# A four-layer gated cross-attention kernel: the first feed-forward layer keeps the inner values of three pairs of tiles instead of two

## The chip, the cores and the metric

The kernel runs on one core of a Trainium2 chip. The metric is the device time of one execution, in microseconds (us). The engines of the core work side by side, each through its own list of instructions in order, and meet only at semaphores: TensorE (PE in the rows; PEld is its weight load), VectorE (DVE), ScalarE (ACT), GpSimd (POOL), and the queue of SyncE that issues transfers (SPq).

## What is computed

The input x is 4 batches of 512 tokens of width 128. Four layers follow one another, and each adds a gated cross-attention over 77 context tokens and then a gated feed-forward part. The change touches the feed-forward part of the first layer alone, whose linear maps quantise both operands to a 4-bit grid in blocks of 16:

```python
def fp4_quant_dequant(x):                      # per block of 16 along the last dim
    scale = max(max|xb| / 6, 1e-12)
    q = GRID[searchsorted(MID, |xb / scale|)] * sign(xb) * scale
def L0_ffn(x, w_gate, w_up, w_down):           # 128 -> 352 -> 128
    gate = fp4_linear(x, w_gate)
    y    = fp4_linear(x, w_up)
    h    = silu(gate) * y
    return fp4_linear(h, w_down)               # h is quantised here
x = x + tanh(g_ffn[0]) * L0_ffn(layernorm(x), ...)
```

## The kernel before, in words

The 2048 tokens are 16 tiles of 128 tokens. The first feed-forward layer (`ffn0`, one function of that name for each of TensorE, ScalarE and VectorE) works on 8 pairs of tiles, j = 0 to 7; i is a tile, i = 2j or 2j + 1. For each pair these steps follow one another:

1. TensorE, `up(i)` (L1747, L1748): the gate values of a tile into bank i % 2 of PSUM, the up values into bank 2 + i % 2. It first waits until the product of the pair before has read the banks (`h_done`).
2. ScalarE, `silu(i)` (L850): the silu of the gate values into `fsg`, one buffer for each tile of a pair.
3. VectorE, `product(j)` (L1326): `h` = up values times silu, for both tiles at once (128 x 704), into `fh[:, j % 2]`; then the maximum of each block of 16 (L1330).
4. VectorE, `rounded(j)`: three small operations for the scales (L981 to L983), and five of 128 x 704 that round to the grid (L973 to L977), from `fh[:, j % 2]` into the work buffer `qh[:, j % 2]`.
5. GpSimd (L677): `qh` times the scale, written back into `fh[:, j % 2]`; it signals `hq_done`.
6. TensorE, `turn(i)` (L1755): three transposes of the tile's part of `fh` into bank 4; it signals `hqT_ps`.
7. ScalarE, `hT_out(i)` (L854, L855): bank 4 into `hqT[:, i % 2]`.
8. TensorE, `down(i)` (L1764): six matmuls that accumulate the output of the tile.

So `fh` has two uses for each pair: VectorE writes the raw values and reads them for the rounding, and then GpSimd puts the quantised values in the same place, from where TensorE transposes them. With two buffers, the product of pair j has to wait until the two tiles of pair j - 2 have been transposed:

```python
dve.wait_ge(silu_done, 2 * j + 2)
if j >= 2:
    dve.wait_ge(hqT_ps, 2 * j - 2)
dve.tensor_tensor(h, ps[:, 2:4, 0:FI], fsg[:, :, :], ALU.mult).then_inc(h_done, 1)
```

The order of work is written out by hand on each engine, by rounds. In round j TensorE issues `up(2j)`, `up(2j+1)`, then `turn(2j-4)`, `down(2j-5)`, `turn(2j-3)`, `down(2j-4)`, so pair j - 2 is transposed behind the up projections of pair j; each `turn` after the first waits until ScalarE has copied the one before out of bank 4. In rounds 5 and 7 the first two batches of the next layer's attention are put in between (a transpose of the input, L1579, and the query projection, L1584). ScalarE issues the two silus of pair j, then the copies of pair j - 2. VectorE issues `product(j)` and `rounded(j)`, and in between: behind the product of pair 1 the quantisation of the last batch's input; behind `rounded(3)` and `rounded(5)` the residual of batch 0 and 1 (L1344, statistics, and a refinement of 1/sqrt); ahead of that of batch 1, and behind the last pair, the low part of the queries (L1207).

Behind the last pair VectorE takes the row maxima of the next layer's attention scores (L1217), 8 units of scores, then the residual of batch 2, 8 more units, and the residual of batch 3. TensorE writes a unit of scores (L1605, L1608, L1609) into bank 0 or 1 in turn, so it is at most two units ahead of the maxima. It issues the first 8 units in round 9, ahead of the last two `turn`s, and the other 8 behind the last `down`.

The buffers live in a region of SBUF that later stages use again. `fh` is followed there by `fsg`, `hqT`, `w1s`, `w2s`, and then by `qh`, whose space is afterwards that of the mask parts `m1hB`, `m1lB` and of `gap2`, a filler that nothing reads. When all of them are given up (`early.close()`), `cT`, `rk1`, `rk2` and the expert weights of the last layer are laid over the same region from its start.

Of the kernel before, what the change touches and what calls it, by code (L numbers as in the profile page):

```python
# [19 lines left out]
P = 128  # L20
# [7 lines left out]
FI = 352  # L28
# [66 lines left out]
def program(nc, a, out):  # L95
    with ExitStack() as ctx:
        def sb(name, shape, dt=F32):
            return ctx.enter_context(nc.sbuf_tensor(name, shape, dt))
# [4 lines left out]
        ps = ctx.enter_context(nc.psum_tensor("ps", [P, 8, 512], F32))  # L103
# [5 lines left out]
        ident = sb("ident", [P, P])  # L109
# [92 lines left out]
        def early_sb(name, shape, dt=F32):  # L202
            return early.enter_context(nc.sbuf_tensor(name, shape, dt))
# [5 lines left out]
        wst = early_sb("wst", [P, 3, 3, P])  # L209
        wqt = early_sb("wqt", [P, 2, FI])  # L210
        wdT = early_sb("wdT", [P, 3, P])
        fh = early_sb("fh", [P, 2, 2, FI])
        fsg = early_sb("fsg", [P, 2, FI])
        hqT = early_sb("hqT", [P, 2, 3, P])
        w1s = early_sb("w1s", [P, F1])
# [2 lines left out]
            qh = lent.enter_context(nc.sbuf_tensor("qh", [P, 2, 2, 2 * FI], F32))  # L218
        m1hB = early_sb("m1hB", [P, 2, S], F32R)
        m1lB = early_sb("m1lB", [P, 2, S], F32R)  # L220
        early_sb("gap2", [P, 768])
        early.close()
        cT = sb("cT", [TPB * NE, 2, P])
        rk1 = sb("rk1", [P, TPB * NE * NE], BF16)
# [274 lines left out]
        def _(pool):  # L499
# [131 lines left out]
            for l in range(L):  # L631
                for k in range(-2, B + 1):
                    n = l * B + k
                    if l == 0 and k == 1:
                        quantise_begun(2)
                        quantise_ended(2)
                    if 0 <= k < B and n + 2 < N and n + 2 >= 3 * B:
                        mask_rows(n + 2)
                    if 0 <= k < B and n + 3 < N:
                        key_rows(n + 3)  # L640
                    if 0 <= k + 1 < B:
                        split_maxima(n + 1)
                    if l == 0 and k == 0:
                        for j in range(2):
                            quantise_begun(j)
                            quantise_ended(j)
                    if l == 0 and k >= 2:
                        quantise_begun(k + 1)
                        quantise_ended(k + 1)
                    if l == 2 and k == -1:  # L650
                        refine((5, B - 1))
                        shift((5, B - 1))
                    if l == 2 and k == -1:
                        pool.wait_ge(am_w_part, 1)
                        pool.partition_all_reduce(am[:, 3:4], am[:, 1:2], P, RMAX).then_inc(am_w_all, 1)
                    if l == 0 and k in (-1, 1, 3):
                        mask_parts((k + 1) // 2)
                    if l == 1 and k in (-1, 0, 2):
                        mask_parts((3, 4, 0, 5)[k + 1])
                    if l == 1 and k == 1:  # L660
                        last_masks()
                    if l == 2 and k == 0:
                        split_experts(gH, gL, 0)
                    if l == 2 and k == 1:
                        split_experts(uH, uL, 1)
                    if k >= 1:
                        refine((2 * l + (l > 1) + 1, k - 1))
                        if l == 0:
                            shift((1, k - 1))
                    if l == 3 and 1 <= k <= 3:  # L670
                        split_down(k - 1)
                if l == 0:
                    for j in range(T // 2):
                        h = fh[:, j % 2, :, :].rearrange("p t (n e) -> p (t n) e", e=16)
                        v = qh[:, j % 2, 0, :].rearrange("p (n e) -> p n e", e=16)
                        pool.wait_ge(hq_scaled, j + 1)
                        pool.tensor_tensor(h, v, hscale[:, j % 2, :].unsqueeze(2).to_broadcast([P, 44, 16]),  # L677
                                           ALU.mult).then_inc(hq_done, 1)
                if l == 1:
                    for m in LN_ORDER[4 * B:6 * B]:  # L680
                        if m not in OWN and m != (5, B - 1):
                            refine(m)
                            shift(m)
                if l == 2:
                    pool.wait_ge(am_part, 1)
                    pool.partition_all_reduce(am[:, 2:3], am[:, 0:1], P, RMAX).then_inc(am_all, 1)
                if l == 3:
                    for n, (b, e) in enumerate(STEPS):
                        if e < NE:
                            k = b * NE + e  # L690
                            pool.wait_ge(s3_done, n + 1)
                            pool.wait_ge(cb_in[k % CRING], 16 * (k // CRING + 1))
                            pool.tensor_tensor(sg[:, n % 3, :], sg[:, n % 3, :], cb[:, k % CRING, :], ALU.mult).then_inc(sc_done, 1)  # L693
# [274 lines left out]
        def _(dve):  # L968
# [10 lines left out]
            def quant_scales(s, inv):  # L979

                link(dve.tensor_scalar(s, s, 1.0 / 6.0, 1e-12, ALU.mult, ALU.max))  # L981
                link(dve.reciprocal(inv, s))
                return dve.tensor_scalar(inv, inv, 1.0 - 2.0 ** -22, None, ALU.mult)  # L983
# [335 lines left out]
            def ffn0(q_rest, maximum):  # L1319
                def product(j):  # L1320

                    h = fh[:, j % 2, :, :]
                    dve.wait_ge(silu_done, 2 * j + 2)
                    if j >= 2:
                        dve.wait_ge(hqT_ps, 2 * j - 2)
                    dve.tensor_tensor(h, ps[:, 2:4, 0:FI], fsg[:, :, :], ALU.mult).then_inc(h_done, 1)  # L1326
                    dve.wait_ge(h_done, j + 1)
                    if j >= 2:
                        dve.wait_ge(hq_done, j - 1)
                    link(dve.tensor_reduce(hscale[:, j % 2, :], h.rearrange("p t (n e) -> p (t n) e", e=16), AX_X, ALU.max,  # L1330
                                           apply_absolute_value=True))

                def rounded(j):

                    v = fh[:, j % 2, :, :].rearrange("p t (n e) -> p (t n) e", e=16)
                    w = [qh[:, j % 2, i, :].rearrange("p (b e) -> p b e", e=16) for i in range(2)]
                    link(quant_scales(hscale[:, j % 2, :], qs[:, 1, :]))
                    quant_steps(w, v, qs[:, 1, :].unsqueeze(2).to_broadcast([P, 44, 16])).then_inc(hq_scaled, 1)
                    dve.wait_ge(hq_scaled, j + 1)
# [161 lines left out]
        def _(pe):  # L1501
# [227 lines left out]
            def ffn0(turn_input, queries, scores):  # L1729
# [20 lines left out]
                def turn(i):  # L1750
                    pe.wait_ge(hq_done, i // 2 + 1)
                    if i >= 1:
                        pe.wait_ge(hqT_ready, i)
                    for c, (f0, fw) in enumerate(FQ):
                        ins = pe.transpose(ps[0:fw, 4, c * P:(c + 1) * P], fh[:, i // 2 % 2, i % 2, f0:f0 + fw], ident[:, :])  # L1755
                    ins.then_inc(hqT_ps, 1)

                def down(i):
# [250 lines left out]
```

## Time and profile before

| What | us |
|---|---|
| Median of 3 runs | 832.74 (832.41 to 835.34) |
| The profiled execution, its own time | 834.32 |
| Its span, from the first to the last instruction | 832.5 |
| VectorE busy | 543.0 (65% of the span) |
| TensorE matmul busy | 638.8 (77%) |
| ScalarE busy | 326.1 (39%) |
| GpSimd busy | 261.4 (31%) |
| The first feed-forward layer: the product of pair 0 starts | 137.93 |
| The last of its products starts | 208.40 |

The mean clock that TensorE was granted is 0.844 of full speed (2.4 GHz); it has two levels, 1.0 and 0.5 (1.2 GHz), and a slice between them holds some of each. In a row of a timeline, the bracket at the end says how long the engine was idle before the instruction and what ended that; "x3" behind a row is that many instructions in one row, with the time of all of them together. Ends of matmuls are modelled. A row of the waits says who waited for whom, how long in total, how many times, and how long at most.

### The profile page before, as it was taken

What the parts mean: (1) busy time and instruction counts of PE and PEld (TensorE: products, weight loads), DVE (VectorE), ACT (ScalarE), POOL (GpSimd) and SP (SyncE); (2) the same over time, 40 slices, a digit from 0 to 9 for tenths busy, and PEclk for the clock granted to TensorE, in tenths of its full rate; (3) what the DMA queues carried; (4) which work ended last, traced back from release to release, by engine and by line L of the source; (5) the groups of instructions that cost most, each with busy time, mean ns of one, the idle gap of its engine ahead of it and who ended that gap; (6) DMA issues with size and microseconds to landing.
All of it is one profiled execution on the core that took longest, in us unless ns stands there. A gap on an engine that the chain in (4) does not pass through costs nothing. (4 is left out here: it accounts for less than half of the span.)

```text
span 832.5 us, 9949 instructions
## 1 busy us (share of the span) xinstructions
PE 638.8 (77%) x2926; PEld 397.5 (48%) x2926; DVE 543.0 (65%) x1451; ACT 326.1 (39%) x627; POOL 261.4 (31%) x470
## 2 busy tenths in 40 slices
PE   5788775566779998884888870348887898989997
PEld 3433333354665564552534330124343576767875
DVE  8775635888772553485736655863558798878655
ACT  3044552233224344353143440214544455545554
POOL 4343365111011312113250721001122445445463
PEclk9577987688869999896599985555998899999999
DMA  8864311002204323006044320222500232333341
GB/s 253 187 177 132 73 37 46 2 0 64 63 12 140 90 41 91 1 1 182 9 123 156 57 76 0 62 64 67 169 6 2 63 103 93 103 113 106 112 121 57
DMA packets 67989, 67.71 MB, mean 81 GB/s; under 512 B 25119, under 2 KB 48223, under 8 KB 67552
## 3 DMA queue, kind: packets, MB, share of 16 engines
q1 hardware_dynamic: 61326, 64.61, 28.4%
q10 hardware_dynamic: 6610, 2.47, 1.2%
q8 instruction: 24, 0.39, 0.2%
q14 instruction: 29, 0.24, 0.1%
HBM read 50.29 MB, written 17.60 MB: 82 GB/s over the span
## 5 line engine op out<-in xcount | busy, mean ns | idle before, releaser
L783 ACT ACTIVATE PT<-ps 110x512 f32<-110x512 f32 x192 | 110.5, 595 | 137.3 <-PE ps L1645 63.4
L1217 DVE TENSOR_REDUCE mraw<-ps 128x4 f32<-128x308 f32 x256 | 116.0, 476 | 73.6 <-PE ps L1605 23.7
L1605 PE MATMUL ps<-KG,QG 98*128 98x308 f32 x256 | 113.0, 477 | 49.4 <-DVE mraw L1217 34.1
L693 POOL TENSOR_TENSOR sg<-sg,cb 128x512 f32<-128x512 f32 x64 | 83.8, 1312 | 78.3 <-ACT sg L945 74.9
L1605 PEld LDWEIGHTS ps<-KG,QG 98*128 98x128 f32 x256 | 59.2, 237 | 94.4 <-DVE mraw L1217 70.4
L1645 PE MATMUL ps<-QG,KG 128*110 128x512 f32 x192 | 93.1, 506 | 9.1 <-ACT PT L783 6.7
L1461 DVE TENSOR_TENSOR ps<-ps,sg 128x512 f32<-128x512 f32 x72 | 50.3, 698 | 39.3 <-POOL sg L693 36.3
L1665 PE MATMUL ps<-PT,VN 128*18 128x512 f32 x512 | 73.0, 644 | 0.0
L525 POOL CAST mhl<-mraw 128x64 fp32r<-128x64 f32 x16 | 5.0, 310 | 192.7 <-DVE mraw L1217 180.0
L945 ACT ACTIVATE sg<-ps 128x512 f32<-128x512 f32 x72 | 43.0, 597 | 46.4 <-PE ps L1864 45.7
L1645 PEld LDWEIGHTS ps<-QG,KG 128*110 128x110 f32 x192 | 35.0, 187 | 54.4 <-ACT PT L783 38.8
L932 ACT ACTIVATE hH<-ps 128x512 fp32r<-128x512 f32 x72 | 43.0, 597 | 37.7 <-DVE ps L1461 36.2
L582 POOL TENSOR_TENSOR nt<-nhv,rs 128x4 f32<-128x4 f32 (+1 forms) x63 | 14.8, 236 | 129.9 <-DVE rs L1057 126.6
L1107 DVE RECIPROCAL rden<-ps 128x32 f32<-128x32 f32 x32 | 11.3, 354 | 64.3 <-PE ps L1555 64.2
L1453 DVE TENSOR_TENSOR hL<-ps,hH 128x512 fp32r<-128x512 f32 x72 | 49.0, 681 | 0.7 <-ACT hH L932 0.6
L724 ACT ACTIVATE xn<-x,nsh,rs 128x128 f32<-128x128 f32 x64 | 26.3, 482 | 44.2 <-DVE nsh L1072 22.4
L1747 PE MATMUL ps<-wqt,xnT 128*128 128x352 f32 x32 | 19.0, 690 | 28.8 <-DVE fh L1326 28.1
L1882 PE MATMUL ps<-hH,dwH 128*128 128x512 f32 x72 | 29.7, 413 | 1.2 <-ACT hH L932 1.2
L677 POOL TENSOR_TENSOR fh<-qh,hscale 128x704 f32<-128x704 f32 x8 | 11.1, 1385 | 59.6 <-DVE qh L977 59.6
L1884 PE MATMUL ps<-hL,dwH 128*128 128x512 f32 x72 | 29.3, 406 | 0.0
L1883 PE MATMUL ps<-hH,dwL 128*128 128x512 f32 x72 | 29.2, 405 | 0.0
L1079 DVE TENSOR_SCALAR xn<-x,mv,rs 128x128 f32<-128x128 f32 x64 | 22.3, 412 | 9.5 <-POOL rs L585 9.4
(284 smaller groups left out, 1414.9 us busy)
## 6 DMA issues: line engine op xcount, KB each, us to landing
cb<-c_parts SPq DMA_DIRECT2D x64, 256.0 KB, 3.3
QG<-q_parts SPq DMA_DIRECT2D x48, 256.0 KB, 3.9
KG<-k_parts SPq DMA_DIRECT2D x48, 154.0 KB, 3.0
q_parts<-hiT SPq DMA_DIRECT2D x14, 256.0 KB, 2.0
q_parts<-loT SPq DMA_DIRECT2D x14, 256.0 KB, 2.3
k_parts<-kmH SPq DMA_DIRECT2D x16, 154.0 KB, 2.4
k_parts<-kmL SPq DMA_DIRECT2D x16, 154.0 KB, 2.6
VN<-v_parts SPq DMA_DIRECT2D x16, 144.0 KB, 2.9
```

Source lines behind the costliest of these rows:

```text
L693: pool.tensor_tensor(sg[:, n % 3, :], sg[:, n % 3, :], cb[:, k % CRING, :], ALU.mult).then_inc(sc_done, 1)
L783: act.activation(PT[0:w, q % PTR, :], ps[0:w, 4 + q % 2, :], ACT.Exp, scale=SCALE[l]).then_inc(exp_done, 1)
L932: act.activation(hH[:, n % 3, :], ps[:, up_bank(n), :], ACT.Copy).then_inc(h_hi, 1)
L945: act.activation(sg[:, n % 3, :], ps[:, n % 2, :], ACT.Silu).then_inc(s3_done, 1)
L1217: dve.tensor_reduce(mraw[:, n % 2, i, g * HG:(g + 1) * HG], ps[:, u % 2, 0:GK].rearrange("p (h k) -> p h k", k=K), AX_X, ALU.max).then_inc ...
L1453: dve.tensor_tensor(hL[:, n % 3, :], ps[:, up_bank(n), :], hH[:, n % 3, :].bitcast(F32), ALU.subtract).then_inc(h_lo, 1)
L1461: dve.tensor_tensor(ps[:, up_bank(n), :], ps[:, up_bank(n), :], sg[:, n % 3, :], ALU.mult).then_inc(a1_done, 1)
L1605: ins = pe.matmul(o, QG[0:KS, n % 3, g, q], KG[0:KS, n % 3, g, :], start=True, stop=l not in (1, 2))
L1645: ins = pe.matmul(o, KG[:, n % 3, g, r], QG[:, n % 3, g, :], start=True, stop=l not in (1, 2))
L1665: pe.matmul(ps[p0:p0 + VC, 6 + f, :], VN[:, n % 3, g * 4 + PAIRS.index((t, j)), :], PT[:, q % PTR, :], start=s == 0, stop=s == 1, skip_gro ...
L1882: pe.matmul(o, dwH[:, e, :], hH[:, r, :], start=e == NE, stop=False)
L1884: pe.matmul(o, dwH[:, e, :], hL[:, r, :], start=False, stop=e == NE - 1).then_inc(f3_step, 1)
```

## The change

`fh` gets a third buffer. The product, the rounding, GpSimd's scaling and the transposes all index it with j % 3 in place of j % 2, and the product of pair j now waits for the transposes of pair j - 3. The work buffer `qh` and the scales stay at two. The filler `gap2` shrinks by the 704 values that `fh` grows by, and all buffers between the two move up by 2816 bytes in each partition.

```diff
-        fh = early_sb("fh", [P, 2, 2, FI])
+        fh = early_sb("fh", [P, 3, 2, FI])
...
-        early_sb("gap2", [P, 768])
+        early_sb("gap2", [P, 64])
...
-                        h = fh[:, j % 2, :, :].rearrange("p t (n e) -> p (t n) e", e=16)
+                        h = fh[:, j % 3, :, :].rearrange("p t (n e) -> p (t n) e", e=16)
...
-                    h = fh[:, j % 2, :, :]
+                    h = fh[:, j % 3, :, :]
                     dve.wait_ge(silu_done, 2 * j + 2)
-                    if j >= 2:
-                        dve.wait_ge(hqT_ps, 2 * j - 2)
+                    if j >= 3:
+                        dve.wait_ge(hqT_ps, 2 * j - 4)
...
-                    v = fh[:, j % 2, :, :].rearrange("p t (n e) -> p (t n) e", e=16)
+                    v = fh[:, j % 3, :, :].rearrange("p t (n e) -> p (t n) e", e=16)
...
-                        ins = pe.transpose(ps[0:fw, 4, c * P:(c + 1) * P], fh[:, i // 2 % 2, i % 2, f0:f0 + fw], ident[:, :])
+                        ins = pe.transpose(ps[0:fw, 4, c * P:(c + 1) * P], fh[:, i // 2 % 3, i % 2, f0:f0 + fw], ident[:, :])
```

## Rows read from the trace of the kernel before

**Rows 1.** Waits, 130 to 240 us: total us, times, longest
```profile
PE ps L1747 <- DVE fh L1326: 28.1, 7, 8.2
...
DVE fh L1326 <- ACT fsg L850: 6.7, 2, 4.2
...
DVE fh L1326 <- PE ps L1755: 4.6, 3, 1.7
```

**Rows 2.** VectorE's timeline, 159 to 209 us: start, duration, line, idle before
```profile
159.84 0.89 DVE L977 TENSOR_TENSOR qh<-qh 128x704 f32<-128x704 f32 x1
160.77 0.89 DVE L1326 TENSOR_TENSOR fh<-ps,fsg 128x704 f32<-128x704 f32 x1
...
166.49 0.89 DVE L977 TENSOR_TENSOR qh<-qh 128x704 f32<-128x704 f32 x1
168.85 0.89 DVE L1326 TENSOR_TENSOR fh<-ps,fsg 128x704 f32<-128x704 f32 x1 [1.47 <-PE ps L1755]
...
188.18 0.89 DVE L1326 TENSOR_TENSOR fh<-ps,fsg 128x704 f32<-128x704 f32 x1 [1.41 <-PE ps L1755]
...
208.40 0.89 DVE L1326 TENSOR_TENSOR fh<-ps,fsg 128x704 f32<-128x704 f32 x1 [1.67 <-PE ps L1755]
```

**Rows 3.** TensorE's timeline: transposes, a down projection, the first delayed scores
```profile
168.20 0.52 PE L1755 MATMUL ps<-ident,fh 128*128 128x128 f32 x3
...
172.66 0.83 PE L1764 MATMUL ps<-wdT,hqT 128*128 128x128 f32 x6
...
207.77 0.49 PE L1755 MATMUL ps<-ident,fh 128*128 128x128 f32 x3
...
216.24 0.63 PE L1605 MATMUL ps<-KG,QG 98*128 98x308 f32 x1 [3.72 <-DVE mraw L1217]
```

**Rows 4.** ScalarE's timeline: the second silu of pair 3 and of pair 7
```profile
166.87 0.46 ACT L850 ACTIVATE fsg<-ps 128x352 f32<-128x352 f32 x1 [1.88 <-PE ps L1748]
...
205.67 0.46 ACT L850 ACTIVATE fsg<-ps 128x352 f32<-128x352 f32 x1 [1.34 <-PE ps L1748]
```

**Rows 5.** GpSimd's timeline: two small operations, then two scalings of the inner values
```profile
139.53 0.20 POOL L583 TENSOR_TENSOR nt<-nt,rs 128x4 f32<-128x4 f32 x1
...
140.69 0.94 POOL L583 TENSOR_TENSOR nt<-nt,rs 128x4 f32<-128x4 f32 x1
...
160.81 1.39 POOL L677 TENSOR_TENSOR fh<-qh,hscale 128x704 f32<-128x704 f32 x1 [13.68 <-DVE qh L977]
167.46 1.39 POOL L677 TENSOR_TENSOR fh<-qh,hscale 128x704 f32<-128x704 f32 x1 [5.26 <-DVE qh L977]
```

**Rows 6.** VectorE's timeline: beside GpSimd, a residual, the row maxima
```profile
140.68 0.89 DVE L973 TENSOR_TENSOR qh<-fh,qs 128x704 f32<-128x704 f32 x1
...
175.51 0.75 DVE L1344 SCALAR_TENSOR_TENSOR x<-ps,tg,x 128x512 f32<-128x512 f32 x1
...
215.72 0.85 DVE L1217 TENSOR_REDUCE mraw<-ps 128x4 f32<-128x308 f32 x2
217.42 0.48 DVE L1217 TENSOR_REDUCE mraw<-ps 128x4 f32<-128x308 f32 x1 [0.85 <-PE ps L1609]
...
219.13 0.48 DVE L1217 TENSOR_REDUCE mraw<-ps 128x4 f32<-128x308 f32 x1 [0.46 <-PE ps L1609]
...
226.63 0.86 DVE L1217 TENSOR_REDUCE mraw<-ps 128x4 f32<-128x308 f32 x2
227.89 0.91 DVE L1217 TENSOR_REDUCE mraw<-ps 128x4 f32<-128x308 f32 x2 [0.40 <-PE ps L1609]
```

**Rows 7.** Slices of 5 us: busy time by engine, granted clock, DMA
```profile
210.00:215.00 5.00, 2.46 (x19) 2.05 (x18) 4.72 (x9) 0.87 (x4) 0.00 (x0) 1.00 0.05 17
215.00:220.00 5.00, 3.76 (x13) 3.39 (x14) 3.07 (x8) 0.00 (x0) 1.39 (x1) 0.52 0.25 83
...
225.00:230.00 5.00, 3.54 (x19) 2.86 (x19) 3.59 (x14) 1.65 (x4) 0.00 (x0) 0.88 0.00 0
...
245.00:250.00 5.00, 4.71 (x28) 3.85 (x27) 3.12 (x7) 2.48 (x3) 0.07 (x1) 1.00 0.00 0
```

## The prediction

> **What bounds the kernel now.** I first took the list of waits for the stretch of the first feed-forward layer, to see which engine keeps the others waiting [rows 1]. TensorE waits 28.1 us for the product on VectorE, in 7 pieces; VectorE waits for others only 6.7 us (ScalarE's silu, twice) and 4.6 us (TensorE's transposes, three times). So the layer is a chain on VectorE with five holes in it, and whatever shortens VectorE's list shortens the layer. The change can touch only the 4.6 us.
>
> The second view is VectorE's timeline, to see where the three holes are [rows 2]. They stand before the products of pair 3 (1.47 us), pair 5 (1.41) and pair 7 (1.67), and each row names the transpose, L1755, as what ended it. The product of pair 2 shows the other case: the operation before it ends at 159.84 + 0.89 = 160.73 and it starts at 160.77, so without a wait the gap is 0.04 us. Pairs 4 and 6 have a residual before their product, which gives the transposes time, and show no wait. The two waits on ScalarE are those of pairs 0 and 1, where the code has no wait for transposes; they stay.
>
> The third view is TensorE's timeline, to check that the named releaser is the right one [rows 3]. The second transposes of pair 1 end at 168.20 + 0.52 = 168.72, and the product of pair 3 follows 0.13 us later. Those of pair 5 end at 207.77 + 0.49 = 208.26, and the product of pair 7 follows 0.14 us later. Two equal lags mean that this is the wait that ends last.
>
> **The change, part by part.** *The wait for transposes.* Pair j now waits for the transposes of pair j - 3, which were issued a whole round earlier: for pair 3 those of pair 0, while the rows show even pair 1's done by 168.72. It never binds. What is late next is the silu of the pair's second tile. For pair 3 it ends at 166.87 + 0.46 = 167.33 [rows 4], and VectorE comes free at 168.85 - 1.47 = 167.38 [rows 2]: a margin of 0.05 us, so the hole closes to the normal 0.04 us, or at worst to 0.1. For pair 7 the silu ends at 205.67 + 0.46 = 206.13 and VectorE is free at 208.40 - 1.67 = 206.73, a margin of 0.6 us; the up projections that feed it start at the product of pair 6, so both move together when the earlier holes close. The gains are 1.47 - 0.04 = 1.43 us, 1.41 - 0.04 = 1.37 us and 1.67 - 0.04 = 1.63 us. Sum: 4.43 us.
>
> *What else VectorE meets once it is early.* The maximum behind each product also waits for `hq_done` of pair j - 2 (its scale buffer has two parts). For pair 3 that is the scaling of pair 1, done at 160.81 + 1.39 = 162.20 [rows 5], 5 us before it is needed: nothing. The residual of batch 0 needs the down projection of tile 3, which ends at 172.66 + 0.83 = 173.49 [rows 3]; the residual starts at 175.51 [rows 6] and would start at 175.51 - 1.43 = 174.08, still 0.59 us behind, and the projection itself moves forward a little. Nothing.
>
> *GpSimd's write beside the product.* Today the scaling of pair 2 (167.46 to 168.85) runs mostly while VectorE is idle [rows 2, 5]. After the change it runs beside the product and the maximum of pair 3. The price is on record already: the scaling of pair 1 runs from 160.81 beside the product of pair 2 at 160.77, and both take what they take alone, 1.39 and 0.89 us. So I take nothing. That the two engines can get in each other's way does show elsewhere: a GpSimd operation of 0.20 us takes 0.94 us when it starts at 140.69 beside VectorE's L973 at 140.68, which reads two operands from SBUF [rows 5, 6]. The Trainium skill (SBUF — State Buffer, "Who interferes with whom") gives the rule for this: a VectorE instruction with two SBUF inputs contends with a GpSimd instruction that reads SBUF, and the one that starts second waits for the whole of the other. By that rule the product, which reads PSUM and SBUF, is free of it, and the trace agrees (0.89 us beside GpSimd's 1.39).
>
> *The buffers that move.* They keep their shapes. The two present buffers of `fh` lie 2816 bytes apart, the distance by which the others move, and products into either take 0.89 us [rows 2]. Nothing.
>
> *What follows the layer.* VectorE's first row maxima start at 215.72 right behind its own work and find two units of scores waiting: TensorE had been idle 3.72 us when it went on at 216.24, since 212.52 [rows 3, 6]. TensorE's work there hangs on the product of pair 6, which moves by 1.43 + 1.37 = 2.80 us, so these units are done at 212.52 - 2.80 = 209.72, and VectorE comes at 215.72 - 4.43 = 211.29. The margin stays at 1.57 us: all 4.43 us reach the attention.
>
> There one term is open, TensorE's clock. Its idle time before it resumes shrinks from 3.72 to 216.24 - 4.43 - 209.72 = 2.09 us. The slice 210 to 215 is at the full 2.4 GHz though the last work ended at 212.52, so 2.48 us of idleness did not lower it; the slice 215 to 220 is at 0.52, all but at 1.2 GHz [rows 7]. At the low clock two units of scores pace the maxima at 219.13 - 217.42 = 1.71 us, at the high clock at 227.89 - 226.63 = 1.26 us [rows 6], 0.45 us less. Six units, three pairs, follow before TensorE turns to other work: the bound above is 3 x 0.45 = 1.35 us, the bound below nothing, and I reckon nothing as a loss here because less idleness does not lower a clock. The slice 225 to 230, at 0.88, shows that the full clock is lost again under such thin work, so I take one pair of three, 0.45 us. The Trainium skill (TensorE: Matmul & The Clock Gate, "HAM oscillation") also says that idle gaps beyond some length put the array back to half rate; by it the shorter gap would keep the clock and the term would be the whole 1.35 us.
>
> *The sum.* 4.43 + 0.45 = 4.88 us. The profiled execution took 834.32 us in all, of which 832.5 is the span; it becomes 829.4. It lies 1.58 us above the median of 832.74, so for the median I forecast 832.74 - 4.88 = 827.9 us. Behind the maxima everything hangs, engine by engine, on what was shifted: the residuals, the masks, the transfers and the later layers are released by semaphores of these engines, so I count no slack that would swallow the gain.
>
> A measurement of this kernel can tell about 0.5% from no change, which is 4.2 us: a gain below 828.6 us counts as faster, so this forecast lies just beyond the mark.
>
> **The rivals.** *The gain is partly swallowed.* If the margin of 0.05 us at pair 3 is really a wait, or the scores turn out late for VectorE at the end, then one hole stays. The largest is pair 7's 1.63 us: 4.43 - 1.63 = 2.80 us remain, 829.9 us. For it: later stages have waits of their own, and a shift of a few us meets transfers at other moments. Against it: the 1.57 us of margin worked out above. Chance 0.18.
>
> *The product runs into GpSimd's write.* Were VectorE held until the scaling ends, pair 3's product would start at 167.46 + 1.39 = 168.85 [rows 5], which is to the hundredth where it starts today [rows 2], and pairs 5 and 7 likewise within about 0.2 us; the gain would be nil, 832.7 us. Against it stands pair 2, whose product ran beside the same operation. Chance 0.04.
>
> *The change does not do what it says.* The wait on `hqT_ps` could be in front while a second one ends at the same time behind it, for instance a bank of PSUM that the silu releases later than the modelled ends say. Then VectorE waits as long as now: 832.7 us. Chance 0.05.
>
> *Slower through TensorE's clock.* The attention behind the layer runs on TensorE at the full clock with hardly a gap: in the slice 245 to 250 it is busy 4.71 of 5 us at 1.00 [rows 7]. If the new arrival times of the work let the clock rise later there, or fall once more, each slice of this kind at 1.2 GHz costs up to another 4.71 us. It decides the sign from 4.43 / 4.71 = 0.94 slices on; two such slices cost 9.42 us and leave 832.74 - 4.43 + 9.42 = 837.7 us. For it: the clock already switches often in this stretch. Against it: the work arrives in the same order with less idleness. Chance 0.04.
>
> *More than the sum.* The clock also comes up sooner behind the maxima: a further 2 us would give 825.5 us. Chance 0.07.
>
> **How the numbers follow.** The forecast with its bounds, 832.74 - 4.43 - 1.35 = 827.0 to 832.74 - 4.43 = 828.3 us, has the remaining chance, 0.62. With 0.07 for more, that makes 0.69 below the mark; because the upper bound is only 0.3 us from it and three runs scatter by more than that, I move 0.05 to no change. Faster by over 0.5%: 0.64. Within 0.5%: 0.32. Slower: 0.04. The range takes in the forecast, the partly swallowed case and some of the scatter: 825.5 to 831.0 us. The nil cases and the slower one, 0.13 together, lie outside.
>
> **What would show each step.** In the changed kernel's timeline the products of pairs 3, 5 and 7 should have no bracket for L1755, and start near 167.4, 185.4 and 204.0 us (if everything before is unchanged). The waits should have no row of the product for the transposes. The first row maxima should start near 211.3 us. GpSimd's scaling should stay at 1.39 us. If the idle time of TensorE before the third unit is near 2.1 us and its clock there is 1.0, the open term is at its upper end. The prediction is wrong if VectorE now waits for the silus (L850) in those three places, or if the maxima start at 211.3 but a later mark, such as the residual of batch 3, has lost the gain again.

## The result, and the profile after

| What | before | after |
|---|---|---|
| Median of 22 executions each, on the same chips, us | 833.98 | 829.48 |
| Ratio, after to before | | 0.9939 (0.9917 to 0.9962) |
| The profiled execution, us | 834.32 | 828.43 |
| Its span, us | 832.5 | 826.6 |
| From the product of pair 2 to that of pair 7, us | 47.63 | 43.20 |
| From there to the residual of batch 3, us | 23.75 | 22.06 |

The kernel is 0.61% faster by this ratio (0.38 to 0.83%), 5.1 us of 833.98. The ratio leaves out the executions in the slower of the two states that every kernel shows now and then; the plain medians differ by 4.50 us. The forecast was 4.88 us, and 827.9 us against a median of 832.74. Two more comparisons, below, gave 0.20 and 0.49%.

The waits of the changed kernel between 130 and 240 us. The row of the product for the transposes [rows 1] is gone, and only the wait for the silus is left:

```profile
PE ps L1747 <- DVE fh L1326: 24.4, 5, 7.9
...
DVE fh L1326 <- ACT fsg L850: 6.6, 2, 3.9
```

VectorE's timeline of the changed kernel: an end of a rounding, the products of pairs 2, 3, 5 and 7, then the first row maxima and the residuals of batches 2 and 3 (L1344):

```profile
163.59 0.89 DVE L1326 TENSOR_TENSOR fh<-ps,fsg 128x704 f32<-128x704 f32 x1
...
169.31 0.89 DVE L977 TENSOR_TENSOR qh<-qh 128x704 f32<-128x704 f32 x1
170.25 0.89 DVE L1326 TENSOR_TENSOR fh<-ps,fsg 128x704 f32<-128x704 f32 x1
...
188.19 0.89 DVE L1326 TENSOR_TENSOR fh<-ps,fsg 128x704 f32<-128x704 f32 x1
...
206.79 0.89 DVE L1326 TENSOR_TENSOR fh<-ps,fsg 128x704 f32<-128x704 f32 x1
...
214.11 0.85 DVE L1217 TENSOR_REDUCE mraw<-ps 128x4 f32<-128x308 f32 x2
215.47 0.48 DVE L1217 TENSOR_REDUCE mraw<-ps 128x4 f32<-128x308 f32 x1 [0.50 <-PE ps L1609]
...
219.61 0.74 DVE L1344 SCALAR_TENSOR_TENSOR x<-ps,tg,x 128x512 f32<-128x512 f32 x1
...
228.85 0.74 DVE L1344 SCALAR_TENSOR_TENSOR x<-ps,tg,x 128x512 f32<-128x512 f32 x1
```

The products of pairs 3, 5 and 7 have no bracket. That of pair 3 starts 0.05 us behind the rounding (169.31 + 0.89 = 170.20). This execution reached the product of pair 2 at 163.59 in place of 160.77 [rows 2], so all places are compared from there: pair 3 stands 6.66 us behind it (8.08 before), pair 5 24.60 (27.41), pair 7 43.20 (47.63), the first maximum 50.52 (54.95). That is 1.42, 2.81, 4.43 and 4.43 us: the three holes, one after another, and nothing lost on the way to the attention.

TensorE's timeline (the second transposes of pair 1, the first up projection behind them, and the first and the last matmul of the third unit of scores), ScalarE's (the second silus of pairs 3 and 7) and GpSimd's (the scalings of pairs 2 and 4):

```profile
171.06 0.49 PE L1755 MATMUL ps<-ident,fh 128*128 128x128 f32 x3
...
172.05 0.76 PE L1747 MATMUL ps<-wqt,xnT 128*128 128x352 f32 x2
...
214.63 0.41 PE L1605 MATMUL ps<-KG,QG 98*128 98x308 f32 x1 [2.16 <-DVE mraw L1217]
...
215.02 0.40 PE L1609 MATMUL ps<-rep,m1lA 128*128 128x308 f32 x1
```

```profile
169.69 0.46 ACT L850 ACTIVATE fsg<-ps 128x352 f32<-128x352 f32 x1 [1.88 <-PE ps L1748]
...
205.63 0.47 ACT L850 ACTIVATE fsg<-ps 128x352 f32<-128x352 f32 x1 [1.27 <-PE ps L1748]
```

```profile
170.28 1.39 POOL L677 TENSOR_TENSOR fh<-qh,hscale 128x704 f32<-128x704 f32 x1 [5.27 <-DVE qh L977]
...
188.23 1.39 POOL L677 TENSOR_TENSOR fh<-qh,hscale 128x704 f32<-128x704 f32 x1 [9.91 <-DVE qh L977]
```

The transposes of pair 1 still end behind the start of the product of pair 3, at 171.55, but now it does not matter. The silu of pair 3 ends at 170.15, 0.05 us before VectorE is free. The up projections of pair 4 follow from 172.05 at the high clock. GpSimd's scalings start 0.03 and 0.04 us behind the products of pairs 3 and 5 and run beside them, and both sides keep their 1.39 and 0.89 us. The Trainium skill's rule (SBUF — State Buffer, "Who interferes with whom"), by which a product with one SBUF input is free of GpSimd, is borne out once more.

Behind the layer there is a second, smaller gain. The residuals of batches 2 and 3 of the kernel before, from the same view, to set beside 219.61 and 228.85:

```profile
222.01 0.74 DVE L1344 SCALAR_TENSOR_TENSOR x<-ps,tg,x 128x512 f32<-128x512 f32 x1
...
232.15 0.74 DVE L1344 SCALAR_TENSOR_TENSOR x<-ps,tg,x 128x512 f32<-128x512 f32 x1
```

From the product of pair 7 to the residual of batch 2 it was 222.01 - 208.40 = 13.61 us and is 219.61 - 206.79 = 12.82; from there to that of batch 3 it was 10.14 and is 9.24. TensorE was idle only 2.16 us before the third unit of scores (3.72 before, [rows 3]) and started it at the high clock (0.41 us for L1605 against 0.63). The clock fell within the next 0.6 us all the same: the last matmul of that unit, at 215.02, takes 0.40 in place of 0.31, the granted clock is 0.50 from 215.2 to 218.3, and it is 1.00 again from 218.7 on. The two parts, 0.79 and 0.90 us, add up to 1.69 us. So between the product of pair 2 and the residual of batch 3 the profiled executions differ by 71.38 - 65.26 = 6.12 us.

### The profile page after: what moved, and what is told of

The parts are those of the page before. It is cut to its first block and busy times, and to the rows that moved or that the text cites. A ratio compares the mean times of both kernels' runs of the same rounds, so it can differ in the third digit from the quotient of the medians.

```text
span 826.6 us, 9949 instructions
## 1 busy us (share of the span) xinstructions
PE 635.7 (77%) x2926; PEld 395.6 (48%) x2926; DVE 540.1 (65%) x1451; ACT 326.6 (40%) x627; POOL 262.4 (32%) x470
## 5 line engine op out<-in xcount | busy, mean ns | idle before, releaser
L1605 PE MATMUL ps<-KG,QG 98*128 98x308 f32 x256 | 112.9, 478 | 49.5 <-DVE mraw L1217 32.8
L1605 PEld LDWEIGHTS ps<-KG,QG 98*128 98x128 f32 x256 | 59.2, 237 | 94.8 <-DVE mraw L1217 70.2
L724 ACT ACTIVATE xn<-x,nsh,rs 128x128 f32<-128x128 f32 x64 | 26.3, 483 | 42.2 <-POOL nsh L596 21.6
L1050 DVE BATCH_NORM_STATS2 st<-x 128x6 f32<-128x128 f32 x128 | 27.9, 280 | 1.2 <-DMA x<-in_x 0.2
```

What stands on the lines that cost most here:

```text
L1605: ins = pe.matmul(o, QG[0:KS, n % 3, g, q], KG[0:KS, n % 3, g, :], start=True, stop=l not in (1, 2))
```

## The experiments

Where the profiles are compared, a stretch is the difference of two starts on VectorE: products of pairs 0, 2 and 7 (p0, p2, p7), residuals of batches 2 and 3 (r2, r3). One execution of each kernel was profiled; the ratio is to the kernel before on the same chip.

| Kernel | p0 to p2 | p2 to p7 | p7 to r2 | r2 to r3 | p2 to r3 | ratio (95% interval) |
|---|---|---|---|---|---|---|
| before | 22.84 | 47.63 | 13.61 | 10.14 | 71.38 | 1 |
| before, again | 22.58 | 47.89 | 13.61 | 10.07 | 71.57 | 0.9983 (0.9954 to 1.0013) |
| three buffers, old wait | 22.28 | 48.17 | 13.60 | 9.23 | 71.0 | 1.0028 (0.9995 to 1.006) |
| old wait but for pair 3 | 24.54 | 47.05 | 13.60 | 10.02 | 70.67 | one execution |
| after | 22.57 | 43.20 | 12.82 | 9.24 | 65.26 | 0.9939 (0.9917 to 0.9962) |
| after, control | 24.53 | 43.18 | 11.91 | 9.23 | 64.32 | 0.998 (0.9952 to 1.0007) |
| after, second control | 22.59 | 43.21 | 12.82 | 9.24 | 65.27 | 0.9951 (0.9912 to 0.999) |
| after, silus first | 19.54 | 43.17 | 13.06 | 9.23 | 65.46 | 0.9969 (0.9931 to 1.0006) |
| two buffers, silus first | 19.24 | 48.07 | 13.61 | 10.03 | 71.71 | 0.9954 (0.9922 to 0.9987) |
| two buffers, TensorE fed | 22.56 | 43.16 | 12.83 | 10.17 | 66.16 | 0.996 (0.9928 to 0.9992) |
| three buffers, fed | 22.24 | 43.16 | 11.94 | 10.02 | 65.12 | 0.9952 (0.9916 to 0.9987) |
| three, silus first, fed | 21.51 | 43.17 | 12.71 | 9.22 | 65.1 | 0.9892 (0.9845 to 0.9938) |
| the same, again | 19.21 | 43.20 | 11.93 | 10.18 | 65.31 | 0.987 (0.98 to 0.9939) |
| two, silus first, fed | 19.21 | 43.20 | 11.94 | 10.23 | 65.37 | 0.9885 (0.9836 to 0.9934) |

In three of these profiles (only pair 3 relieved, the first control, and the first of the kernels with everything together) the product of pair 0 waits 0.60 us for its silu in place of 2.5 to 3.0, so it starts sooner against the work behind it, and the stretch from p0 to p2 is some 2 us longer. That moves the mark and need not be a loss.

### The third buffer with the old wait

```diff
-                    if j >= 3:
-                        dve.wait_ge(hqT_ps, 2 * j - 4)
+                    if j >= 2:
+                        dve.wait_ge(hqT_ps, 2 * j - 2)
```

> The third buffer is there and everything behind it in the region has moved, but the product waits for the transposes of pair j - 2 as before. Theory (the wait is the whole cause): the holes of about 1.5 us before the products of pairs 3, 5 and 7 are back, the stretch from the product of pair 2 to the product of pair 7 is 47.6 us as in the kernel before, and the time is that of before within 0.4%. Rival (the place of the buffers matters, or the buffer itself frees something): the stretch or the whole stays shorter, by up to the 5 us gained, with the holes back.

The holes are back and the time is that of before within its interval (0.9995 to 1.006). So the wait is the cause of the gain, and nothing shows that the memory or the shifted buffers do anything. But the holes are not the same ones, and the stretch is 48.17 us, not the 47.6 expected. VectorE's products of pairs 2, 3, 5 and 7:

```profile
168.54 0.89 DVE L1326 TENSOR_TENSOR fh<-ps,fsg 128x704 f32<-128x704 f32 x1
...
175.54 0.89 DVE L1326 TENSOR_TENSOR fh<-ps,fsg 128x704 f32<-128x704 f32 x1 [0.39 <-PE ps L1755]
...
195.93 0.89 DVE L1326 TENSOR_TENSOR fh<-ps,fsg 128x704 f32<-128x704 f32 x1 [2.50 <-PE ps L1755]
...
216.71 0.89 DVE L1326 TENSOR_TENSOR fh<-ps,fsg 128x704 f32<-128x704 f32 x1 [2.22 <-PE ps L1755]
```

They are 0.39, 2.50 and 2.22 us, where the kernel before had 1.47, 1.41 and 1.67 [rows 2]. TensorE's up projections of pair 3 (from 169.57) and of pair 5 (from 187.85) say why:

```profile
169.57 1.51 PE L1747 MATMUL ps<-wqt,xnT 128*128 128x352 f32 x2 [4.22 <-DVE fh L1326]
...
172.05 1.16 PE L1747 MATMUL ps<-wqt,xnT 128*128 128x352 f32 x2
173.05 0.76 PE L1748 MATMUL ps<-wqt,xnT 128*128 128x352 f32 x2
...
187.85 1.51 PE L1747 MATMUL ps<-wqt,xnT 128*128 128x352 f32 x2 [5.96 <-DVE fh L1326]
...
190.33 1.38 PE L1747 MATMUL ps<-wqt,xnT 128*128 128x352 f32 x2
191.51 1.38 PE L1748 MATMUL ps<-wqt,xnT 128*128 128x352 f32 x2
```

Each pair has four such groups of two, two groups for each tile. A group takes 1.38 us where the granted clock is 0.50 (169.6 to 172.0, and 187.9 to 192.6) and 0.76 where it is 1.00. In pair 3 the clock rises in the third group (1.16) and the hole is 0.39; in pair 5 no group is fast, and the hole is 2.50. So the hole seems to be as long as the clock is late; the table under "The kernel before against itself" tests that on all the profiles.

### Only pair 3 relieved

```diff
-                    if j >= 3:
+                    if j == 3:
                         dve.wait_ge(hqT_ps, 2 * j - 4)
+                    elif j >= 2:
+                        dve.wait_ge(hqT_ps, 2 * j - 2)
```

> Three buffers, but only the product of pair 3 waits for the older transposes; pairs 5 and 7 wait as before. Theory (three separate holes that add): no hole at pair 3, holes of 1.41 and 1.67 us at pairs 5 and 7, and the stretch from the product of pair 2 to that of pair 7 is 47.63 - 1.42 = 46.2 us. Rival (slack is handed on, so that one hole eats the gain of the other): the holes at pairs 5 and 7 grow to take back part of the 1.42 us, and the stretch stays above 46.6 us.

VectorE's products of pairs 3, 5 and 7 (two lines lower in this file):

```profile
176.23 0.89 DVE L1328 TENSOR_TENSOR fh<-ps,fsg 128x704 f32<-128x704 f32 x1
...
196.11 0.89 DVE L1328 TENSOR_TENSOR fh<-ps,fsg 128x704 f32<-128x704 f32 x1 [1.98 <-PE ps L1757]
...
216.62 0.89 DVE L1328 TENSOR_TENSOR fh<-ps,fsg 128x704 f32<-128x704 f32 x1 [1.95 <-PE ps L1757]
```

The hole of pair 3 is closed, to 6.66 us exactly, but the other two are 1.98 and 1.95 us, and the stretch is 47.05, not 46.2. By its numbers that is what the rival said (the gain taken back further on), and the theory, which had the sizes fixed, falls. But the run above had larger holes with nothing relieved before them, so the size need not be slack handed on. In pair 5 the first three groups of the up projections are slow and the fourth takes 1.15, and the hole is as long as such a late clock makes it (the table below). Whether relieving pair 3 made the clock rise later is not shown. There is one execution of this kernel, of 849.24 us, and its time is not used.

### The changed kernel as its own control

> The changed kernel once more, on the same chip as the others. Theory: pairs 2 to 7 in 43.2 us, 4.43 less than before, in every profile; the time 0.5 to 0.7% below before. Rival (part of the measured gain was scatter of the clock further on): the stretch is the same 43.2 us, and the whole comes out only 0.3 to 0.5% below, or up to 1.0%.

> The changed kernel a third time, because the first comparison gave 0.6% and the second 0.2%. Theory (both are the same gain of 4.5 to 6 us, read through scatter of single executions): 43.2 us from the product of pair 2 to that of pair 7, about 65 us from the product of pair 2 to the residual of batch 3 against 71.4 before, and a ratio between 0.993 and 0.998. Rival (part of the gain is given back behind the layer): the stretch from the residual of batch 3 to the end is longer than the 600.4 us before by 2 us or more, and the ratio is 0.998 or above.

The stretch is 43.18 and 43.21 us, as it was 43.20. The ratios, 0.9980 and 0.9951, beside 0.9939, scatter far more than that: single executions of the changed kernel lie between 822 and 841 us. The 0.5 to 0.7% that the theory expected of the first control did not come, nor did its rival's: it gave 0.20%, with an interval of -0.07 to 0.48%. Weighted by their intervals, the three comparisons make 0.45%, or 3.8 us, give or take 1.3 (an estimate from the three ratios). On the chip of the first control the kernel with the third buffer and the old wait ran as well. Twelve executions of it average 837.6 us and twelve of the control 833.3: 4.3 us, give or take 2.4, for the wait alone. The rival's sign of a gain given back does show in both controls: from the residual of batch 3 to the end it is 602.7 and 606.1 us, against 600.4 before; but 597.7 in the first profile of the changed kernel. In the other kernels with the old wait, wholly or in part, the same tail is 595.5 to 607.2 us. The four kernels with the old wait throughout and nothing added on TensorE average 598.0 us, and the four with the new one 601.4, a difference that profiles so far apart cannot tell from scatter.

How far the gain can be followed shows where VectorE reads the last output of the next layer's attention, before and after:

```profile
335.73 0.69 DVE L1227 TENSOR_TENSOR yb<-ps,rows 128x512 f32<-128x512 f32 x1 [2.00 <-PE ps L1567]
```

```profile
332.57 0.69 DVE L1227 TENSOR_TENSOR yb<-ps,rows 128x512 f32<-128x512 f32 x1 [2.18 <-PE ps L1567]
```

From the product of pair 2 to there it is 335.73 - 160.77 = 174.96 us before, and 174.57 to 174.96 in all four profiles with the old wait and nothing added; in the three of the changed kernel it is 168.98, 169.08 and 169.05. So 5.5 to 6.0 us reach the end of the next layer's attention every time. In the first control the maxima had gained more (64.32 us to the residual of batch 3), and the attention took that back: 104.76 us from there, against 103.58 before and 103.72 and 103.78 in the other two. What the remaining 490 us do with the gain stays open.

### The kernel before against itself

> The kernel before against itself. Both theories: a ratio of 1.000; how far it is from that shows what 12 runs can tell. Its profile gives the holes once more: theory (the holes follow where the clock rises within the up projections of the pair) 0.3 to 2.5 us each and 46.5 to 48.5 us in all from pair 2 to pair 7, and 71 us to the residual of batch 3. Rival (the holes are fixed at 1.5 us): 47.6 us again.

0.9983: twelve executions can be off by 0.17% with nothing changed. Its holes are 1.48, 1.58 and 1.74 us, the stretch 47.89: near the first profile, and not the spread that the theory allows. With the others, the old wait on all pairs has 47.63 to 48.17 us in four profiles, the new one 43.17 to 43.21 in four without added matmuls.

Five profiles, of four kernels, have holes. For each, this is the group of the pair's up projections in which the clock rises, with the time of that group, and then the hole on VectorE, all in us:

| Profile | pair 3 | pair 5 | pair 7 |
|---|---|---|---|
| before | behind all four groups: 1.47 | third, 1.16: 1.41 | fourth, 0.84: 1.67 |
| before, again | behind all four: 1.48 | third, 1.33: 1.58 | fourth, 0.91: 1.74 |
| two buffers, silus first | behind all four: 1.53 | fourth, 0.84: 1.68 | fourth, 0.97: 1.80 |
| old wait but for pair 3 | relieved | fourth, 1.15: 1.98 | fourth, 1.12: 1.95 |
| three buffers, old wait | third, 1.16: 0.39 | behind all four: 2.50 | behind all four: 2.22 |

Within each pair the hole grows with every step by which the clock is later, without an exception. (The three at 1.47 to 1.53 us are in order too: the down projection behind the first transposes takes 0.90, 1.06 and 1.18 us.) Between pairs the sizes differ for the same clock, since in pairs 5 and 7 TensorE has a transpose of the input and a query projection ahead of the second transposes. The holes of one and the same kernel, in its two profiles, differ by 0.01 to 0.17 us; the wide spread is between kernels.

### The silus of pair 1 ahead of the normalisation

```diff
-                    if j == 0:
+                    if j == 1:
                         normalise_out((1, B - 1))
```

In ScalarE's `ffn0`; the call stands behind the silus of its round. First what it goes against, ScalarE's timeline in the changed kernel: the second silu of pair 0, the normalisation (L724) behind an idle time that GpSimd ends, and the two silus of pair 1 behind that:

```profile
140.52 0.46 ACT L850 ACTIVATE fsg<-ps 128x352 f32<-128x352 f32 x1 [1.52 <-PE ps L1748]
148.63 1.65 ACT L724 ACTIVATE xn<-x,nsh,rs 128x128 f32<-128x128 f32 x4 [7.65 <-POOL nsh L596]
...
150.66 0.79 ACT L850 ACTIVATE fsg<-ps 128x352 f32<-128x352 f32 x2
```

> The changed kernel, with ScalarE's normalisation of the last batch issued behind the silus of pair 1 in place of ahead of them. Theory (the 3.9 us hole before the product of pair 1 is ScalarE standing at GpSimd's shift with the silus queued behind it): the hole goes, the product of pair 1 runs right behind the rounding of pair 0, and VectorE instead waits about 1 us for the normalised input before it quantises the last batch; 2.5 to 3.5 us less than the changed kernel in the stretch from the product of pair 0 to that of pair 2. Rival (the quantisation of the last batch is what binds, and it needs the same normalisation): the wait only changes its place, and at most 1 us is gained.

VectorE's products of pairs 0 and 1 in the new kernel, and the quantisation of the last batch (L1098):

```profile
145.05 0.89 DVE L1326 TENSOR_TENSOR fh<-ps,fsg 128x704 f32<-128x704 f32 x1 [2.72 <-ACT fsg L850]
...
151.74 0.89 DVE L1326 TENSOR_TENSOR fh<-ps,fsg 128x704 f32<-128x704 f32 x1
...
154.43 0.69 DVE L1098 TENSOR_REDUCE qs<-xn 128x32 f32<-128x512 f32 x1 [0.88 <-ACT xn L724]
```

The product of pair 1 has no bracket and comes 6.69 us behind that of pair 0 (10.54 in the changed kernel); the wait appears again at L1098 with 0.88 us. From p0 to p2 it is 19.54 us against 22.57: 3.0 us less, as the theory had it. The ratio is 0.9969, which cannot be told from that of the controls. That is less than the profile promises: from p0 to the residual of batch 3 it is 85.00 us, where the kernel before has 94.22, but the whole gains 2.6 us, at most 5.8 by the interval. A part of it goes in the next attention, 105.28 us against 103.58; where the rest goes is not shown.

> The kernel before (two buffers) with only the silus of pair 1 ahead of the normalisation of the last batch. Theory (independent of the third buffer): 19.5 us from the product of pair 0 to that of pair 2, and 47 to 48 us from pair 2 to pair 7 with the three holes in place; 0.3 to 0.5% below before. Rival (the two changes feed on the same slack): the stretch from pair 2 on grows by what the first one loses.

The same edit on two buffers gives 19.24 us and leaves the three holes (48.07 us). In these stretches the two changes do not touch each other. Its ratio, 0.9954, is no worse than that of the two changes together.

### TensorE kept busy where it stood idle

```diff
+                def keep_busy(done, count):
+                    pe.wait_ge(hqT_ready, done)
+                    for _ in range(count):
+                        pe.matmul(ps[:, 4, :], ident[:, :], xnT[:, 0, :], start=True, stop=True)
...
+                    if j in (3, 5, 7):
+                        keep_busy(2 * j - 4, {3: 5, 5: 6, 7: 7}[j])
                     if j < T // 2:
                         up(2 * j)
```

The added matmuls write the bank of the transposes, which is free there.

> The kernel before (two buffers), with 5, 6 and 7 matmuls of 128x512 whose result nothing reads, issued on TensorE ahead of the up projections of pairs 3, 5 and 7, where it stood idle for 4.7 to 7.1 us. Theory (the holes exist only because the up projections run at 1.2 GHz behind that idleness, so that the transposes behind them come late): with the clock held at 2.4 GHz the up projections of a pair take 2.4 us in place of 4.8, the transposes end before VectorE is free, and the holes before the products of pairs 3, 5 and 7 go with two buffers: 43.2 to 43.8 us from the product of pair 2 to that of pair 7. Rival (the holes come from the order of the work, whatever the clock): the stretch stays at 47 to 48 us, or is longer if the added matmuls delay the up projections.

This is the kernel before, with two buffers and the old wait. TensorE's timeline, with the added matmuls (L1774), two groups of the up projections of pair 3, and the second transposes of pair 1; then VectorE's products of pairs 2, 3, 5 and 7:

```profile
161.91 4.46 PE L1774 MATMUL ps<-xnT,ident 128*128 128x512 f32 x10
166.53 0.83 PE L1747 MATMUL ps<-wqt,xnT 128*128 128x352 f32 x2 [0.16 <-DVE fh L1326]
...
167.79 0.75 PE L1747 MATMUL ps<-wqt,xnT 128*128 128x352 f32 x2
...
170.22 0.52 PE L1755 MATMUL ps<-ident,fh 128*128 128x128 f32 x3
```

```profile
165.50 0.89 DVE L1326 TENSOR_TENSOR fh<-ps,fsg 128x704 f32<-128x704 f32 x1
...
172.15 0.89 DVE L1326 TENSOR_TENSOR fh<-ps,fsg 128x704 f32<-128x704 f32 x1
...
190.07 0.89 DVE L1326 TENSOR_TENSOR fh<-ps,fsg 128x704 f32<-128x704 f32 x1
...
208.66 0.89 DVE L1326 TENSOR_TENSOR fh<-ps,fsg 128x704 f32<-128x704 f32 x1
```

All three holes are gone, and the stretch is 43.16 us, what the third buffer gives. With the up projections at 0.75 to 0.83 us a group in place of 1.38 (granted clock 1.00 from 166.5 to 171.0), the transposes end at 170.74, and VectorE is free at 172.11. So the order of work alone does not need a third buffer: it takes the low clock for the two buffers to be too few. The ratio, 0.996, agrees with that of the changed kernel.

> The changed kernel with the same added matmuls (5, 6 and 6), and two more between the second and third unit of scores, where it stood idle for 2.2 us. Theory: the stretch from the product of pair 2 to that of pair 7 stays at 43.2 us, since the third buffer has already taken TensorE off the path; the first 8 row maxima run at the pace of the high clock (1.26 us for two) in place of 1.70, so that the residual of batch 3 starts up to 1 us earlier behind the product of pair 7 than in the changed kernel. Rival (the pace of the maxima is set elsewhere): no difference in the second stretch.

Here the third buffer and the added matmuls are together (six in place of seven ahead of pair 7), with two more matmuls ahead of the third unit of scores. The first stretch does not change (43.16 us). The row maxima of this kernel, and the residual of batch 2:

```profile
215.84 0.85 DVE L1217 TENSOR_REDUCE mraw<-ps 128x4 f32<-128x308 f32 x2
217.09 0.91 DVE L1217 TENSOR_REDUCE mraw<-ps 128x4 f32<-128x308 f32 x2 [0.40 <-PE ps L1609]
218.36 0.91 DVE L1217 TENSOR_REDUCE mraw<-ps 128x4 f32<-128x308 f32 x2 [0.35 <-PE ps L1609]
...
220.46 0.74 DVE L1344 SCALAR_TENSOR_TENSOR x<-ps,tg,x 128x512 f32<-128x512 f32 x1
```

Two maxima every 1.26 us throughout, at a granted clock of 1.00 from 216.4 to 220.0, and the residual 11.94 us behind the product of pair 7, 0.88 us sooner than in the first profile of the changed kernel. So the pace of the maxima is the clock's. That the two added matmuls held the clock is not shown: in the first control, with none added, it held as well (11.91 us), and in the first kernel below, with the same two, it fell (12.71). From r2 to r3, where nothing was added, the clock fell again, and it takes 10.02 us: 0.78 lost. At the residual of batch 3 this kernel is only 0.10 us ahead of the changed one (21.96 against 22.06 from the product of pair 7), not the 1 us that the theory allowed.

### All together

Three buffers, the silus first, and the added matmuls of the last kernel, profiled and timed twice; then the same with two buffers and the old wait:

> Three buffers, the silus of pair 1 ahead of the normalisation, and the added matmuls, all together. Theory (the parts add): 19.5 us from the product of pair 0 to that of pair 2 as in the run with the silus first, 43.2 us from pair 2 to pair 7, and the fastest of all, 0.8 to 1.2% below before. Rival (the added matmuls cost clock or time later on): no faster than the run with the silus first alone.

> Three buffers, silus first and added matmuls once more, since the first comparison rests on few runs. Theory (the parts add): 0.8 to 1.2% below before. Rival (the first result was a lucky draw): 0.4 to 0.6% below before, as each part alone.

> The same, with two buffers and the old wait in place of three: silus first and the added matmuls. Theory (with the clock held, the third buffer has nothing left to take away): no holes, 43.2 us from the product of pair 2 to that of pair 7, and the time of the run with three buffers within 0.3%. Rival (the third buffer helps beside the clock): holes remain, 1 us or more each, and the time is 0.3% or more above.

The ratios are 0.9892, 0.9870 and 0.9885, from six executions each, so the intervals are wide, but they lie below those of the changed kernel, by 4 to 9 us, depending on which two are compared. In the first of them the quantisation waits 2.32 us for the normalised input, so p0 to p2 is 21.51 us; in the others it is 19.21. With two buffers there is no hole either (VectorE, the products of pairs 2, 3 and 7):

```profile
165.62 0.89 DVE L1326 TENSOR_TENSOR fh<-ps,fsg 128x704 f32<-128x704 f32 x1
...
172.27 0.89 DVE L1326 TENSOR_TENSOR fh<-ps,fsg 128x704 f32<-128x704 f32 x1
...
208.82 0.89 DVE L1326 TENSOR_TENSOR fh<-ps,fsg 128x704 f32<-128x704 f32 x1
```

The last kernel does this without the third buffer's 2816 bytes in each partition; on its chip it averages 6.3 us less than the changed kernel, give or take 3.7. With the third buffer, the silus first and the feeding, the gain is 1.1 to 1.3% against the 0.8 to 1.2% expected, which agrees within the intervals. That the parts add in general is not shown: without the feeding, the silus first and the third buffer gave 0.31% together (above).

## Why the prediction was right

- **What bounds the layer.** Right. VectorE's list is the chain, and the 4.6 us of waits for the transposes are all that the change takes away [rows 1].
- **The sum of the holes.** The forecast was 1.43 + 1.37 + 1.63 = 4.43 us. The profiles differ by 1.42, 1.39 and 1.62, 4.43 in all. That it fits to the hundredth is partly luck: in its second profile the kernel before has 1.48, 1.58 and 1.74 us, and the same wait has holes of 0.39 to 2.50 us in other kernels. The four kernels with the old wait throughout average 47.94 us and the four with the new wait, unfed, 43.19, so the typical term is 4.75 us.
- **The next wait.** Right, with the margin of 0.05 us at pair 3 found again. It can hardly get smaller: all four groups of pair 3's up projections were already at the low clock there.
- **No cost at GpSimd, in the moved buffers, in the scales and residuals.** Right as far as the runs tell; the run with the old wait bears out the second, within its interval.
- **The clock behind the layer.** This term was too small, 0.45 us. From the product of pair 7 to the residual of batch 2 it measured 0.79 us in the first profile, 1.70 and 0.79 in the controls. The 1.70 lies above the bound of 1.35: the bound counts the steps from one pair of maxima to the next and leaves out the last one, from the last pair to the residual, which the high clock shortens by another 0.35 us (1.17 to 0.82). The second eight maxima, which the prediction did not count, gave another 0.90. They do not need the change for it, since the third buffer with the old wait has 9.23 us from r2 to r3 as well. But that is one of five profiles with the old wait on some pair and nothing added, and with the new wait it is all four, so whether the change makes the high clock likelier there is open. The argument that 2.48 us of idleness had not lowered the clock did not carry far: after 2.16 us the work started fast and was slow 0.6 us later.
- **Everything reaches the end.** Shown as far as the next layer's attention, and not to the end. The layer and the start of the attention gain 6.1 us between the two profiles and 6.3 on average (71.41 against 65.08 us from p2 to r3, four profiles each), and 5.5 to 6.0 us are left where that attention ends; the whole gained 5.1, 1.7 and 4.1 us in three comparisons, 3.8 together. Each comparison is uncertain by 2 to 3 us, and so is the tail, so this is either scatter or a give-back of 1 to 3 us. If there is one, the forecast of 4.88 us owes part of its fit to it: the stages that were looked at gained more than was counted.
- **The rivals.** GpSimd's write, a change without effect and a slower clock later on did not happen. A gain partly swallowed further on is not excluded, but no hole stayed in the places that were named.

What the prediction lacked is the layer below its reasons. It took the late transposes for a matter of order, read the lag of 0.13 us rightly, and did not ask why the transposes were late. TensorE's timeline of the kernel before has the answer: the first up projections of pairs 3, 4 and 7.

```profile
161.81 1.51 PE L1747 MATMUL ps<-wqt,xnT 128*128 128x352 f32 x2 [4.74 <-DVE fh L1326]
...
169.89 0.83 PE L1747 MATMUL ps<-wqt,xnT 128*128 128x352 f32 x2 [0.50 <-DVE fh L1326]
...
201.15 1.51 PE L1747 MATMUL ps<-wqt,xnT 128*128 128x352 f32 x2 [7.07 <-DVE fh L1326]
```

Before the odd pairs 3, 5 and 7 TensorE stood idle for 4.7 to 7.1 us and started the up projections at half rate (granted clock 0.50 from 161.8 to 166.6); before pair 4 it stood idle for 0.50 us and ran them at the full one. The Trainium skill (Perfetto Trace Analysis, "Identifying Performance Opportunities") says that the same gap repeating on the engine that should be saturated can mean too few buffers; this trace agrees, since a third one closed the gaps. The Trainium skill (TensorE: Matmul & The Clock Gate, "HAM oscillation") tells of a kernel whose bursts of matmuls each start at the low clock behind an idle gap, and advises to arrange the work so that TensorE stays at the high one. The fed kernel with two buffers agrees with that, at 43.16 against 43.20 us.

## What to carry to other kernels

When an engine waits for a buffer to come free, look at how fast the one who frees it runs at that moment: here a third buffer and a few idle matmuls each removed the same 4.4 to 5.0 us, because it took the low clock and two buffers together to make the wait. The stretch with the new wait came out within 0.04 us in four profiles, while the whole kernel needs dozens of executions to show 0.6%; compare starts of named instructions from a common one. And a hole that an in-order engine causes by standing at a third party's result (the silus behind the normalisation, 3 us) is removed by moving one line; how much of that reaches the end has to be measured in the whole.

## What was not expected of the hardware

- With the same wait, the hole before the product of pair 3 was 0.39 to 1.53 us, and that of pair 5 1.41 to 2.50, since the granted clock rises at other points of the work in other kernels. A single profile gives one draw of such a term.
- TensorE's clock fell during thin work behind 2.16 us of idleness in the changed kernel (215.0 us), and behind 1.32 us, some 2 us into the work, in the first of the kernels with everything together. It held through the same work behind 1.32 us in the kernel with three buffers and the added matmuls.
- The up projections of pair 4 started slow behind 1.77 us of idleness in the kernel with three buffers and the added matmuls (1.49 us for the first group) and fast behind 1.78 us in the one with two (0.83). So the length of the gap ahead does not decide it alone.
- Added matmuls on an idle TensorE cost nothing that these runs show; the three kernels with all of them and the silus first have the lowest ratios.
